# Cross-attention and a routed FFN on one core: 64-row array tiles for both score products, and the weighted values of two key tiles made together

## What is computed

```python
q = (layernorm(x) @ Wq + bq)          # 16 heads of 16
k = (ctx @ Wk + bk); v = (ctx @ Wv + bv)
scores = einsum('bnhd,bmhd->bhnm', q, k) / 4
out = einsum('bhnm,bmhd->bnhd', softmax(scores), v)
x = x + tanh(g0) * (relu(out @ W1 + b1) @ W2 + b2)
x = x + tanh(g1) * (shared(layernorm(x)) + sum over the top 2 of 8 experts)
```

## Time and profile before

| | |
|---|---|
| median of 3 runs | 1333.47 us (1330.21 to 1335.7) |
| profiled execution, its span (the only time there is of it) | 1354.8 us |
| of it attention | about 935 us |
| PE busy | 1254.9 us, 93% |
| DVE busy | 749.8 us, 55% |
| ACT busy | 546.8 us, 40% |
| mean granted TensorE clock | 0.958 of 2.4 GHz |

### The profile page before, as it was taken

One profiled execution on the slowest core, in us unless ns is written; L12 is line 12 of the kernel. 1 busy time (PEld: TensorE's weight loads), 2 busy tenths in 40 slices (PEclk: granted clock), 3 DMA queues, 4 the chain that ended last, 5 costly groups with the idle time before them and its releaser, 6 DMA issues. The chain is left out here.

```text
span 1354.8 us, 16247 instructions
## 1 busy us (share of the span) xinstructions
PE 1254.9 (93%) x5662; PEld 704.1 (52%) x5662; DVE 749.8 (55%) x1624; ACT 546.8 (40%) x1004; POOL 97.3 (7%) x114
## 2 busy tenths in 40 slices
PE   6899999999999999999999999997858999999982
PEld 2455545555645555554555565544434555555551
DVE  1498776686776588576668778632601222222244
ACT  1006564564555366346456547771201111111110
POOL 4000000000000000000000000000170000000044
PEclk9959999999999999899999999997988999999996
DMA  9344403323210453040322421010850111111124
GB/s 308 45 68 71 53 1 47 63 37 51 28 26 1 53 90 49 5 53 1 41 32 34 53 30 24 5 51 4 297 184 31 32 46 40 39 48 39 39 71 124
DMA packets 53840, 78.43 MB, mean 58 GB/s; under 512 B 13312, under 2 KB 38912, under 8 KB 53760
## 3 DMA queue, kind: packets, MB, share of 16 engines
q1 hardware_dynamic: 47744, 67.01, 24.9%
q0 software_dynamic: 3072, 8.39, 1.9%
q10 hardware_dynamic: 2944, 1.98, 0.5%
HBM read 32.47 MB, written 16.52 MB: 36 GB/s over the span
## 5 line engine op out<-in xcount | busy, mean ns | idle before, releaser
L442 ACT ACTIVATE probs<-st_ps 128x512 f32<-128x512 f32 (+1 forms) x832 | 450.5, 598 | 361.8 <-PE st_ps L542 360.6
L677 DVE TENSOR_REDUCE mpart<-ring 128x1 f32<-128x402 f32 x1024 | 521.3, 568 | 85.0 <-PE ring L488 83.0
L488 PE MATMUL ring<-kst,qst 128*128 128x402 f32 x1024 | 389.1, 406 | 0.8 <-DVE xnT L637 0.3
L542 PE MATMUL st_ps<-qst,kst 128*128 128x512 f32 (+1 forms) x832 | 327.7, 400 | 1.9 <-ACT probs L442 1.8
L488 PEld LDWEIGHTS ring<-kst,qst 128*128 128x128 f32 x1024 | 200.1, 196 | 215.1 <-DVE mpart L677 175.9
L554 PE MATMUL pv_ps<-probs,vp 128*17 128x512 f32 (+1 forms) x1664 | 219.6, 600 | 0.1
L542 PEld LDWEIGHTS st_ps<-qst,kst 128*128 128x128 f32 (+1 forms) x832 | 154.0, 187 | 41.8 <-ACT probs L442 19.5
L845 ACT ACTIVATE s_sb<-gu_ps 128x512 f32<-128x512 f32 x55 | 32.9, 598 | 304.8 <-PE gu_ps L920 252.5
L920 PE MATMUL gu_ps<-wgu,xbT 128*128 x312 | 144.1, 604 | 7.4 <-issue 7.3
L1049 DVE TENSOR_TENSOR h_sb<-s_sb,gu_ps 128x512 f32<-128x512 f32 x55 | 37.8, 687 | 204.0 <-ACT s_sb L845 184.0
L920 PEld LDWEIGHTS gu_ps<-wgu,xbT 128*128 128x128 f32 x312 | 56.1, 189 | 78.5 <-issue 78.5
(11 more groups left out here) (125 smaller groups left out, 716.2 us busy)
## 6 DMA issues: line engine op xcount, KB each, us to landing
kst<-parts SPq DMA_DIRECT2D x192, 100.2 KB
qst<-parts SPq DMA_DIRECT2D x192, 32.0 KB
sorted_x<-zeros SPq DMA_DIRECT2D x1, 4992.0 KB, 16.4
xb<-sorted_x SPq DMA_DIRECT2D x39, 128.0 KB, 2.1
sorted_y<-ysb SPq DMA_DIRECT2D x39, 128.0 KB, 1.7
wgu<-in_WgT SPq DMA_DIRECT2D x16, 256.0 KB, 6.7
wgu<-in_WuT SPq DMA_DIRECT2D x16, 256.0 KB, 7.1
wd<-in_WdT SPq DMA_DIRECT2D x8, 512.0 KB, 8.4
```

The costliest lines, as they stand in the source:

```text
L442: nc.scalar.activation(probs[0:w, m % NPB, h, :], st_ps[0:w, (4 * m + h) % NST, :], ACT.Exp, scale=SCALE).then_inc(exp_done, 1)
L488: last = nc.tensor.matmul(slot[:, 0:SCH], qst[u % NKB][:, h, t * P:(t + 1) * P], kst[u % NKB][:, h // 2, score_at(q):score_at(q) + SCH], s ...
L542: nc.tensor.matmul(st_ps[0:w, idx % NST, :], kst[u % NKB][:, h // 2, mt * P:mt * P + w], qst[u % NKB][:, h, :], start=True, stop=True).the ...
L677: last = nc.vector.tensor_reduce(mpart[:, h, t, q:q + 1], slot[:, 0:SCH], AX.X, ALU.max)
```

## The change

- S and T take only the 48 (49) partitions of their head, at partition 0 or 64, so that each product uses a tile of 64 rows of the array. The order of the S chunks alternates between the two heads of a pair, and PE's order in a step is two S, two T, two S, two T, the rest of the S, PV, other jobs.
- `qst` has one column block for two heads, and the row of zeros goes, with its DMA and its memsets.
- PV is issued for two steps at once at even steps; step 12's comes alone at step 0 of the next unit. `NPB` is 3.

```diff
-NPB = 2
+NPB = 3
     def scores(u):
-        return [("S", u, h, t, q) for h in range(4) for t in range(NT) for q in range(4)]
+        return [("S", u, 2 * p + j, t, q) for p in range(2) for t in range(NT) for q in range(4) for j in range(2)]
-        qst = [sb(f"qst{i}", [P, 4, N], F32R) for i in range(NKB)]
-        zrow = sb("zrow", [4, P])
+        qst = [sb(f"qst{i}", [P, 2, N], F32R) for i in range(NKB)]
-        STACK_LOADS = 16 * 2 * 7
+        STACK_LOADS = 16 * 2 * 6
-                        sp.dma_start(qst[u % NKB][at:at + 1, 2 * p + j, :].rearrange("o (t n) -> o t n", n=P).bitcast(F32),
-                                     zrow[:]).then_inc(loaded, 16)
-            nc.gpsimd.memset(zrow[:], 0.0)
-                nc.gpsimd.memset(qst[i][:].bitcast(F32), 0.0)
-                    last = nc.tensor.matmul(slot[:, 0:SCH], qst[u % NKB][:, h, t * P:(t + 1) * P],
-                                            kst[u % NKB][:, h // 2, score_at(q):score_at(q) + SCH],
+                    at = 64 * (h % 2)
+                    last = nc.tensor.matmul(slot[:, 0:SCH], qst[u % NKB][at:at + STK, h // 2, t * P:(t + 1) * P],
+                                            kst[u % NKB][at:at + STK, h // 2, score_at(q):score_at(q) + SCH],
...
-                nc.tensor.matmul(st_ps[0:w, idx % NST, :], kst[u % NKB][:, h // 2, mt * P:mt * P + w],
-                                 qst[u % NKB][:, h, :], start=True, stop=True).then_inc(st_full, 1)
+                at = 64 * (h % 2)
+                rows = slice(at, at + STK + 1)
+                nc.tensor.matmul(st_ps[0:w, idx % NST, :], kst[u % NKB][rows, h // 2, mt * P:mt * P + w],
+                                 qst[u % NKB][rows, h // 2, :], start=True, stop=True).then_inc(st_full, 1)
...
-                for h in range(4):
-                    if h == 3 and MT * u + mt > 0:
-                        pv(MT * u + mt - 1)
-                    for job in chunks[h:h + 1]:
-                        do(job)
-                    st(u, mt, h)
-                for job in chunks[4:] + others:
-                    do(job)
+                for p in range(2):
+                    for job in chunks[2 * p:2 * p + 2]:
+                        do(job)
+                    for j in range(2):
+                        st(u, mt, 2 * p + j)
+                for job in chunks[4:]:
+                    do(job)
+                if mt == 0 and u > 0:
+                    pv(MT * u - 1)
+                elif mt > 0 and mt % 2 == 0:
+                    pv(MT * u + mt - 2)
+                    pv(MT * u + mt - 1)
+                for job in others:
+                    do(job)
```

More of the change, by code:

```diff
@@ L311, in load_stacks @@
                                          kc[r:r + HD, dt, kpart, :].bitcast(F32)).then_inc(loaded, 16)
-                            sp.dma_start(qst[u % NKB][at:at + HD, 2 * p + j, :].bitcast(F32),
+                            sp.dma_start(qst[u % NKB][at:at + HD, p, :].bitcast(F32),
                                          qc[r:r + HD, dt, qpart, :].bitcast(F32)).then_inc(loaded, 16)
-                        at = 64 * j + STK
-                        sp.dma_start(qst[u % NKB][at:at + 1, 2 * p + j, :].rearrange("o (t n) -> o t n", n=P).bitcast(F32),
-                                     zrow[:]).then_inc(loaded, 16)
             def load_rows(u):
@@ L323, in load_rows @@
                     at = 64 * (h % 2) + STK
-                    sp.dma_start(qst[u % NKB][at:at + 1, h, :].rearrange("o (t n) -> o t n", n=P).bitcast(F32),
+                    sp.dma_start(qst[u % NKB][at:at + 1, h // 2, :].rearrange("o (t n) -> o t n", n=P).bitcast(F32),
                                  mneg[NT * h:NT * (h + 1), :].bitcast(F32)).then_inc(row_loaded[u % NKB], 16)
```

## The result

The changed kernel takes 1467.11 us (median of 4 runs, 1465.2 to 1471.51) against 1332.74 us (1330.21 to 1335.7) for the kernel before on the same chip: a ratio of 1.100 (95% interval 1.097 to 1.103). The forecast was 1310.5 us with a range of 1294 to 1345: wrong in size and in sign. Of its rivals the one on the clock came true, at a higher price than it was given. (The ratios in this document leave out runs that lie well above the fastest of the same kernel, as one of the four of e2 does.) What follows tells apart two errors. One is the clock, some 120 of the 134 us. The other is smaller: the gain of 23 us is not there even where the clock is at its upper level.

A forecast was written before the change was run, and what follows sets the result against it. The prediction took PE's own sequence as the bound, with DVE close behind. Gains of 11 + 11 + 2.5 less a loss of 1.5 made 23 us, so 1333.5 - 23 = 1310.5 us, range 1294 to 1345.

The forecast's parts named there:

- the one on the clock: Rival, chance 0.14: between PV groups PE's work gets thin, the clock falls; at a third of 93 pairs, 1367 us.
- the gain of 23 us: Whole kernel: 11 from plain units, 11 from W1/W2 units, 2.5 from unit 0, less 1.5 in unit 15.
- What bounds the kernel before: Attention steps: PE's own sequence sets the 3.03 us step, with DVE closely behind.
- Tiles side by side: S and T: two heads' products run at once, at best costing half of 0.216 us each.
- PV for two steps: PV at even steps: the second group adds 0.86 us, saving one way in and out of PV every two steps.
- What DVE sees: Behind each PV pair DVE idles 0.82 us as its slots run out; two steps take 5.65 us against 6.06.
- ACT just keeps out of it: After PE's return the eighth T waits for ACT until 3.49 us; the last S may go at 3.52.
- A plain unit: Units 3, 7, 11, 13, 14: 38.8 us against 41.05, a gain of 2.2 each, 11 us in all.
- Units with K and V: Second and third units of a batch: 59.8 and 61.1 us with K, V, XT and Q jobs; no gain.
- Units with W1 and W2: Three units: jobs cost 16.3, unit 55.1 us against 59.1, `onc` wait gone; 3.7 us gained each, 11 in all.
- Unit 15: Unit without S, where ACT sets the step: pairs take 5.3 us for two steps against 5.18, a loss of 1.5.

The follow-up runs named there:

- e2: The changed kernel with its 64-row tiles (48/49 rows used), but one PV group in every step after S and T; ratio 1.052 to the kernel before.
- e10: The changed kernel with PV at every step and each tile on all 64 rows of its half, extra rows zero; ratio 1.013 to the kernel before.
- e8: As e3, but three score slots in the ring in place of four; ratio 1.052 to the kernel before.
- e3: The kernel before with the new order, PV for two steps and three probs buffers, all products on 128 rows; ratio 1.014 to the kernel before.
- e7: As e3, but S and T issued in turn (S T S T) instead of two and two; ratio 1.004 to the kernel before.
- e9: The changed kernel with each S and T tile on all 64 rows of its half, extra rows zero; ratio 1.049 to the kernel before.
- e5: The kernel before, same order, with every S and T on the lower 48 or 49 rows (odd heads' results wrong); 1683 to 1816 us, no ratio.
- e13: The kernel before, same order, with every S and T on rows 0 to 63 (odd heads' results wrong); ratio 1.125 to the kernel before.
- e12: The kernel before with S alone on 64-row tiles, T on 128 rows, order S S T T, PV at every step; ratio 1.084.
- e11: The kernel before with T alone on 64-row tiles, S on 128 rows, order S S T T, PV at every step; ratio 1.086.

## Why the prediction was wrong, step by step

- **What bounds the kernel before.** Right. With S and T cheaper (e2, e10, upper level) a plain unit is 39.4 to 39.5 us instead of 41.05, and DVE and ACT are waited for.
- **Tiles side by side.** Right: two S in 0.45 us, starts within hundredths.
- **PV for two steps.** PE was forecast back 0.99 + 0.86 = 1.85 us after PV's start; it is 307.13 - 305.29 = 1.84.
- **What DVE sees.** The mechanism was right (e8), the size was not. Idle 0.82 forecast, 0.99 measured; the period 5.65 forecast, 5.96 in e3 and 5.79 in e7. After's own at the upper level is 318.58 - 314.51 = 4.07 us from the return to PV where 3.80 was forecast, so 5.91 with the 1.84. The failed term is the 3.52 us after PE's return at which the last S was to start, with "ACT just keeps out of it". The lines below show it. The eighth T, the second of the two at 317.85, starts at 317.96, 3.45 us after the return; 3.49 was forecast, so ACT was reckoned rightly. The last S then stands behind this T on the same rows and starts at 318.31, at 3.80. PV follows 0.27 us later, as forecast. A margin of 0.03 us between two chains was taken as none waiting for the other, and the last S waits 0.35 us behind the T.
- **A plain unit, 38.8.** 40.3 us at 1.00 with this order (e9, unit 7), 41.1 on 128 rows (e3). Of the 2.2 us, 0.8 remained. Unit 14 was counted as one of five with this gain, but it takes 38.8 us before the change already.
- **Units with K and V.** "No gain" was forecast. e3 has 64.3, 63.7 and 64.2 us in units 1, 5 and 9, where before has 59.8, 58.6 and 59.6, so the forecast is wrong by some 4 us in each of three. The starts of the PV groups of e3 tell the terms apart. In unit 5, less the same stretches of a plain unit, XT and Q cost 9.7 us (10.0 forecast) and the five K 10.5 (10.96 by the prices given): both were about right. What was wrong is the plain unit under them, 41.1 for 38.8, and the count. From COPY to COPY there are six K and not five, as the one in step 0 of the next unit falls in too; it was priced in the third unit, whose 61.1 us thus agree with e3's 60.8 by luck. (Its three K are put at 6.6 us; the prices given make 5.96.) Second and third unit together were forecast at 120.9 us, and units 1 and 2 of e3 take 125.1. Two plain units at 41.1 for 38.8 are 4.6 us, which covers the difference.
- **Units with W1 and W2.** The wait for `onc` went, as forecast: PE waits 0.1 us in all W1 of after's attention. The jobs were priced rightly too: 16.6 us in unit 4 of e3, by the starts of its PV groups, for 16.3. But the unit is 57.8 to 58.6 us in e3, not 55.1, again because the plain unit under it is 41.1 and not 38.8.
- **Unit 15.** A loss of 1.5 forecast, 4.1 in e3. Of this, 2.3 us are in steps 8 to 11, where the jobs `XT2` and `LG` stand, for which the forecast had no price; a stretch of 3.4 us at the lower clock level falls in there too.
- **Together** these terms, the plain unit above all, take the 23 us to nothing and beyond: e3, with the clock up, ends the attention 18 us later than before.
- **The clock.** The step that failed most. The sum had no term for it, and its rival was held down by the argument "each holds full PV work on either side", with a third of the 93 pairs of steps at the lower level as the price. In after, 50 of the 96 pairs of PV groups take over 2.3 us in place of 1.91, and the low time is 323 us in place of 21. The price of one such pair was right (1.7 us: 3.61 at 296.20 in after against 1.91). How often was not, and neither was the reason: the prediction weighed how densely PE started products, by two rows (a prologue at 0.50, unit 15 at 1.00), and S, T and PV have 128 rows in both. What e5 shows in its place is that dense work on 48 rows does not hold the clock. That a product of 48 rows counts for less than one of 128 could not be read from the rows of before, where every S and T stands on 128; it should have stood as an unknown with bounds, and with it the chance of this rival, 0.14, was too low.

The term of the last S rests on these rows of after, behind the return at 314.51:

```profile
317.85 0.61 PE L537 MATMUL st_ps<-qst,kst 49*128 49x512 f32 x2
...
318.31 0.35 PE L481 MATMUL ring<-kst,qst 48*128 48x402 f32 x1
```

The price of a pair at the lower level rests on this row of after, in unit 3:

```profile
296.20 3.61 PE L549 MATMUL pv_ps<-probs,vp 128*17 128x512 f32 x16
```

What stays open: why a run at 64 rows falls for whole units of 40 to 75 us and after falls 53 times for 6 us in the mean. Which quantity the gate weighs is not settled either. Between kernels of the same order, more rows in use always meant less low time (48, 64, 96 and 128 rows; 48 to 64 in the tiles of after and of e2). But the rows and columns of all products together do not settle it. The S and T of e5 and of after have the same, and so have those of e13 and e9, yet one after the other they had 877 and 458 us at the lower level, and side by side 323 and 130. Nor does the work of a unit fix its level: units 2, 6 and 10 of e5 hold the same work, and took 64.2, 63.3 and 111.7 us, with 7, 5 and 112 of them at the lower level. Why was not tested.

## What to carry to other kernels

A product on fewer rows is not only cheaper work for TensorE, it can take the clock from everything behind it: before tiling a small contraction, ask what clock the wide products next to it will then get, and keep rows of zeros where they cost nothing. When two chains meet within hundredths of a microsecond in a sum, take the meeting as a cost and not as a coincidence without price. If a change helps some stages and hurts others, look at the stages one by one: here the pairs in eleven of sixteen units gave 0.5%, and in all of them nothing or a loss (1.004 in e7).

## What the runs showed of the hardware

- TensorE busy for 220 us on end stayed at the lower of its two levels when its score products stood on 48 rows (e5). On 48, 64, 96 and 128 rows, with the same instructions in the same order, the attention had 877, 458, 36 and 21 us at that level.
- Rows that hold zeros in the query stack count as rows in use: 64 rows in place of 48 in each tile brought the changed kernel from 323 to 130 us at the lower level (e9), and e2 from 211 to 62 (e10).
- A change between products on 64-row tiles and on 128 rows costs about 0.16 us (an estimate from e12, after and e3), and the weight load behind it is no longer hidden; with four to six in a step (e11, e12) the kernel was 8% slower.
